# Attention stage of a macaron block: fewer visits to the values, the causal masks one by one, and the sums' copy on another engine

## The reference

```python
x = x + 0.5 * ffn(layernorm(x))        # gate and up 512 -> 4096, tanh GELU, down 4096 -> 512; weights in 4-bit codes
x = x + attention(layernorm(x))        # 16 heads of 32, causal, 2048 tokens
x = x + 0.5 * ffn(layernorm(x))        # the same weights again

# attention, per head:
scores = q @ k.T / sqrt(32) + causal
out = softmax(scores) @ v              # then out @ w_out.T + b_out over all heads
```

## Time and profile before

| | |
|---|---|
| median of the runs | 2957.84 us |
| the profiled execution | 2956.98 us, span 2955.2 us |
| PE busy | 2893.9 us, 98% of the span |
| DVE, ACT, POOL busy | 1826.2, 1051.2, 1066.9 us (62%, 36%, 36%) |
| granted TensorE clock, mean | 0.995 |
| the attention's heads | some 1263 to 1860 us of the span |

### The profile page before, as it was taken

One profiled execution on the slowest core, in us unless ns is written; L12 is line 12 of the kernel. 1 busy time (PEld: TensorE's weight loads), 2 busy tenths in 40 slices (PEclk: granted clock), 3 DMA queues, 4 the chain that ended last, 5 costly groups with the idle time before them and its releaser, 6 DMA issues. The chain is left out here.

```text
span 2955.2 us, 49495 instructions
## 1 busy us (share of the span) xinstructions
PE 2893.9 (98%) x19280; PEld 2336.1 (79%) x19280; DVE 1826.2 (62%) x3321; ACT 1051.2 (36%) x1827; POOL 1066.9 (36%) x745
## 2 busy tenths in 40 slices
PE   7999999999999999999999999899999999999999
PEld 5888888888888877867777776678888888888887
DVE  5665655565656544577777775666565655565664
ACT  4322222222222222266666664432222222222222
POOL 3322222222222214566666662332222222222221
PEclk9999999999999999999999999999999999999999
DMA  3000000000000015732232222100000000000001
GB/s 100 29 22 29 22 28 21 21 24 25 26 23 28 1 47 99 222 86 60 61 74 70 60 85 63 37 29 22 29 24 26 26 24 21 21 28 21 28 8 57
DMA packets 98630, 127.86 MB, mean 43 GB/s; under 512 B 43068, under 2 KB 51244, under 8 KB 95148
## 3 DMA queue, kind: packets, MB, share of 16 engines
q1 hardware_dynamic: 98476, 125.72, 15.1%
HBM read 96.34 MB, written 29.34 MB: 43 GB/s over the span
## 5 line engine op out<-in xcount | busy, mean ns | idle before, releaser
L59 PE MATMUL psum<-ffn_x_high,ffn_w_high 128*128 128x512 f32 x2048 | 800.0, 391 | 15.3 <-DVE ffn_gelu L466 13.2
L60 PE MATMUL psum<-ffn_x_low,ffn_w_high 128*128 128x512 f32 x2048 | 798.0, 390 | 0.0
L61 PE MATMUL psum<-ffn_x_high,ffn_w_low 128*128 128x512 f32 x2048 | 797.8, 390 | 0.0
L612 POOL TENSOR_TENSOR ffn_inner<-ffn_gelu,ffn_inner 128x512 fp32r<-128x512 f32 x256 | 346.1, 1352 | 1156.5 <-ACT ffn_inner L549 1156.5
L456 DVE SCALAR_TENSOR_TENSOR ffn_gelu<-ffn_gelu,psum 128x512 f32<-128x512 f32 x256 | 176.0, 688 | 606.8 <-ACT ffn_gelu L542 606.8
L59 PEld LDWEIGHTS psum<-ffn_x_high,ffn_w_high 128*128 128x128 f32 x2048 | 385.2, 188 | 98.8 <-DVE ffn_gelu L466 16.3
L61 PEld LDWEIGHTS psum<-ffn_x_high,ffn_w_low 128*128 128x128 f32 x2048 | 385.2, 188 | 80.3
L60 PEld LDWEIGHTS psum<-ffn_x_low,ffn_w_high 128*128 128x128 f32 x2048 | 385.3, 188 | 79.6
L59 PE MATMUL psum<-ffn_inner,ffn_w_high 128*128 128x512 f32 x1024 | 398.6, 389 | 0.2
L60 PE MATMUL psum<-ffn_inner,ffn_w_high 128*128 128x512 f32 x1024 | 398.4, 389 | 0.0
L61 PE MATMUL psum<-ffn_inner,ffn_w_low 128*128 128x512 f32 x1024 | 398.3, 389 | 0.0
(11 more groups left out here) (123 smaller groups left out, 3567.1 us busy)
## 6 DMA issues: line engine op xcount, KB each, us to landing
ffn_words<-packed SPq DMA_DIRECT2D x96, 256.0 KB
ffn_word_scales<-scales SPq DMA_DIRECT2D x96, 256.0 KB
qk_parts<-parts SPq DMA_DIRECT2D x32, 512.0 KB, 4.0
queries<-qk_parts SPq DMA_DIRECT2D x48, 256.0 KB, 4.1
keys<-qk_parts SPq DMA_DIRECT2D x48, 256.0 KB, 6.2
v_parts<-parts SPq DMA_DIRECT2D x16, 256.0 KB, 3.0
values<-v_parts SPq DMA_DIRECT2D x16, 256.0 KB, 7.7
out<-x SPq DMA_DIRECT2D x16, 256.0 KB, 2.0
```

Source lines behind the costliest of these rows:

```text
L59: pe.matmul(out, w_high, x_high, start=first, stop=False, skip_group_check=True)
L60: pe.matmul(out, w_high, x_low, start=False, stop=False, skip_group_check=True)
L61: return pe.matmul(out, w_low, x_high, start=False, stop=last, skip_group_check=True)
L612: pool.tensor_tensor(inner[:, tb % 2, m, 1, :], product[m], f32(inner[:, tb % 2, m, 0, :]), ALU.subtract)\
```

## The change

`MEETS_AT` replaces the visit behind each batch by six visits in a head: batches 0 and 1 behind slot 7, 2 and 3 behind slot 15, 4 behind 19, 5 and 6 behind 27, 7 and 8 behind 35, 9 behind 39. `quads` gets a third buffer. Each diagonal tile's mask is issued directly behind its scores. In the 15 heads of `head`, the copy out of `out_bank` moves from ACT to DVE, there behind `take_max` and `split_max` of the same slot; the last head keeps it on ACT, and keeps its ten visits.

```diff
--- before.py
+++ after.py
@@ -673,6 +673,9 @@
 
 QUADS = [i for i in range(BATCHES) if BATCH * i not in DIAGONAL_TILES]
 
+MEETS_AT = {7: (0, 1), 15: (2, 3), 19: (4,), 27: (5, 6), 35: (7, 8), 39: (9,)}
+NQUADS = 3
+
 
 
 
@@ -1288,7 +1291,7 @@
         ROWS, queries, keys, values = heads.ROWS, heads.queries, heads.keys, heads.values
         probs = sb("probs", [P, RING, TB], F32)
         heads_out = sb("heads_out", [P, NOUT, 2, P], F32)
-        quads = sb("quads", [P, 2, TB], F32)
+        quads = sb("quads", [P, NQUADS, TB], F32)
 
         start = sb("start", [P, 7], F32)
 
@@ -1377,9 +1380,9 @@
                 if kt < 4 * b:
                     last.then_inc(scores_ready, 1)
 
-            def masks(s, u):
-                for v in (u - 1, u):
-                    pe.matmul(score_bank_of(s, v)[:, 0:P], heads.ident_b[:], heads.key_mask_b[:],
+            def mask(s, u):
+                if u in DIAGONAL_TILES:
+                    pe.matmul(score_bank_of(s, u)[:, 0:P], heads.ident_b[:], heads.key_mask_b[:],
                               start=False, stop=True, skip_group_check=True).then_inc(scores_ready, 1)
 
             def value_lane(s, t, q):
@@ -1398,7 +1401,7 @@
                 c = QUADS.index(i)
                 pe.wait_ge(quad_steps, 54 * hp + 18 * (s + 1) + 3 * (c + 1))
                 for q in range(QUARTERS):
-                    last = sum_lane(quads[:, c % 2, :], q, 0)
+                    last = sum_lane(quads[:, c % NQUADS, :], q, 0)
                 last.then_inc(quads_met, 1)
 
             def meet_batch(hp, s, i, last_head=False):
@@ -1426,21 +1429,16 @@
                 if t0 + BATCH - 1 in OUT_DONE:
                     last.then_inc(out_ready, 1)
 
-            def masks_of(s, u, in_batch):
-                if u in DIAGONAL_TILES and u % 2 == 1 and (u % BATCH == BATCH - 1) == in_batch:
-                    masks(s, u)
-
             def head(hp, s):
                 for t in range(SLOTS):
                     of, u = divmod(t + AHEAD, SLOTS)
                     scores(hp, s + of, u)
-                    masks_of(s + of, u, False)
+                    mask(s + of, u)
                     heads.max_chunk(pe, hp, s + 1, t)
                     if t in ROWS_AT:
                         heads.rows(pe, hp, s + (ROWS_AT[t] not in OWN_ROWS), ROWS_AT[t])
-                    masks_of(s + of, u, True)
-                    if t % BATCH == BATCH - 1:
-                        meet_batch(hp, s, t // BATCH)
+                    for i in MEETS_AT.get(t, ()):
+                        meet_batch(hp, s, i)
 
             def project(n):
                 k = STEPS[n][1]
@@ -1464,11 +1462,9 @@
                     u = t + AHEAD
                     if u < SLOTS:
                         scores(hp, 0, u)
-                        masks_of(0, u, False)
+                        mask(0, u)
                     if t in ROWS_AT and ROWS_AT[t] in OWN_ROWS:
                         heads.rows(pe, hp, 0, ROWS_AT[t], alone=True)
-                    if u < SLOTS:
-                        masks_of(0, u, True)
                     if t % BATCH == BATCH - 1:
                         for n in STEPS_AT.get(t // BATCH, []):
                             project(n)
@@ -1485,11 +1481,18 @@
 
         @block.vector
         def _(dve):
+            def take_out(hp, s, e):
+                dve.wait_ge(out_ready, 3 * NOUT * hp + (NOUT * s + e + 1))
+                dve.wait_ge(out_stored[e], 240 * hp + 80 * (s + 1))
+                dve.tensor_copy(heads_out[:, e, :, :], out_bank[:, 0:2 * P]).then_inc(out_free, 1)
+
             def head(hp, s):
                 for m in range(SLOTS):
                     heads.take_max(dve, hp, s + 1, m)
                     if m == LAST_CHUNK[CHUNKS[m][0]]:
                         heads.split_max(dve, hp, s + 1, CHUNKS[m][0])
+                    if m in OUT_DONE:
+                        take_out(hp, s, OUT_DONE.index(m))
 
             heads.fill_ones(dve, 2)
             def scale(n):
@@ -1582,18 +1585,12 @@
                 act.wait_ge(out_stored[e], 240 * hp + 80 * (s + 1))
                 act.activation(heads_out[:, e, :, :], out_bank[:, 0:2 * P], ACT.Copy).then_inc(out_free, 1)
 
-            def take_outs(hp, s, t):
-                if t in OUT_DONE:
-                    take_out(hp, s, OUT_DONE.index(t))
-
             def head(hp, s):
                 for t in range(SLOTS):
                     of, u = divmod(t + AHEAD, SLOTS)
                     exps(hp, s + of, u)
                     if t in ROWS_AT:
                         heads.store_rows(act, hp, s + (ROWS_AT[t] not in OWN_ROWS), ROWS_AT[t])
-                    if t % BATCH == BATCH - 1:
-                        take_outs(hp, s, t)
 
             def high(n):
                 act.wait_ge(o.scaled, scaled_at(n))
@@ -1609,7 +1606,8 @@
                     if t % BATCH == BATCH - 1:
                         for n in STEPS_AT.get(t // BATCH + 1, BEHIND[:3]):
                             high(n)
-                        take_outs(hp, 0, t)
+                        if t in OUT_DONE:
+                            take_out(hp, 0, OUT_DONE.index(t))
                 for n in BEHIND[3:]:
                     high(n)
 
@@ -1626,7 +1624,7 @@
         def _(pool):
             def add_quad(hp, s, i):
                 c = QUADS.index(i)
-                total = quads[:, c % 2, :]
+                total = quads[:, c % NQUADS, :]
                 steps = 54 * hp + 18 * (s + 1) + 3 * c
                 tiles = [probs[:, (SLOTS * s + BATCH * i + j) % RING, :] for j in range(BATCH)]
                 pool.wait_ge(quads_met, 18 * hp + (6 * s + c + 1))
@@ -1641,7 +1639,7 @@
             for e in range(NOUT):
                 pool.memset(start[:, e + 1:e + 2], 0.0).then_inc(out_stored[e], 80)
             pool.memset(start[:, 5:6], 0.0).then_inc(quad_steps, 18)
-            pool.memset(start[:, 6:7], 0.0).then_inc(quads_met, 2)
+            pool.memset(start[:, 6:7], 0.0).then_inc(quads_met, NQUADS)
             for hp in range(HEADS // 3):
                 for s in range(3):
                     for i in QUADS:
```

## The result

| | us |
|---|---|
| before, median of six runs (2956.95 to 2958.70) | 2957.56 |
| after, median of six runs (2929.72 to 2930.97) | 2930.38 |
| ratio, 95% interval | 0.9908 (0.9895 to 0.9920) |
| span of the profiled execution, before and after | 2955.2, 2928.9 |

What follows compares the result with a forecast made beforehand. PE, busy 98% of the span, was taken as the bound; stretch terms and DVE's 0.10 summed to -1.09 us a head, -16.4 over 15 heads, giving 2941.5 us; range 2930 to 2955, own range 2932 to 2949.

Steps and rivals of the forecast that it cites:

- rows in mid-stretch: Behind slots 3 and 31: `rows` taken to leave the next score's weights unhidden as a visit does; only 0.10 us each saved.
- row store: ACT's store of 0.58 us between exponentials 3 and 4 delays slot 7's score: about 0.35 lost, bounds 0 and 0.58.
- B: Slots 8 to 15 of a head, 7.10 us before; predicted -0.44: visit -0.31, bubble -0.22, masks +0.09.
- D: Slots 20 to 27 of a head, 7.03 us before; predicted -0.49: visit -0.31, bubble -0.27, masks +0.09.
- E: Slots 28 to 35 of a head, 7.32 us before; predicted -0.48: visit -0.10, bubbles -0.56, masks +0.18.
- A: Slots 0 to 7 of a head, 6.32 us before; predicted +0.25: visit -0.10, row store +0.35.
- The bubble: Waits of 128-wide scores behind mask pairs, in slot 11 and behind 22, 30 and 34: all 1.05 us a head goes.
- C: Slots 16 to 19 of a head, 3.25 us before; predicted change 0.
- 1, the copy held by POOL: DVE's copies wait for POOL's additions behind slots 15, 27, 39: 1.9 us more a head, 2970, slower; chance 0.11.
- 2, ACT holding B and D as well: Exponentials hold slots 4 to 7 of each long stretch, 0.35 again in B and D: 2952; chance 0.10.
- 3, no change: Single masks lose 0.07 more per batch and three quarters of the 1.05 bubbles return: 2958; chance 0.08.
- 4, better than the sum: Row store hides, `rows` leave nothing unhidden, single masks cost only their columns: -2.00 a head, 2928; chance 0.08.

## Why the prediction was right or wrong

**The bound** was right: PE's start-to-start distances carry the time, and no other engine took over. The sum was short by 0.52 a head. The steps below say where; the largest are the rows in mid-stretch (0.30) and DVE's lateness (0.10), and the row store (0.13) goes the other way. What is left in B, D and E (0.04, 0.07, 0.04) is not traced.

**The visits**: 0.31 each was right for slots 11 and 23 (B and D came out at -0.48 and -0.56 for -0.44 and -0.49). For slots 3 and 31 I took rows in mid-stretch to leave the next score's weights as unhidden as a visit does. They don't: from the rows at 1498.12 the score starts 0.23 later, as the rows' own four matmuls take, and its chunk 0.29 behind it where 0.235 is plain. Leaving rows costs 0.06, not 0.21, so 0.25 and not 0.10 goes in A and in E. This is the largest term that I mis-sized, 0.15 in each.

**The masks**: the timeline agrees with 0.13 a single mask (0.04 to the chunk, 0.32 from the chunk on instead of 0.235) and with the four of a batch costing some 0.08 more than two pairs: slots 8 to 11 take 2.09 after, and 2.34 - 0.22 (bubble) - 0.11 (entry) = 2.01 before. **The bubble** of 1.05 went, as the masks alone show (-0.78 in B, D and E together: 1.05 less some 0.3 for the masks' own cost). What I missed is that this term holds up the others: a sum of parts gave the visits a gain that they don't have while the masks come in pairs. It did no harm to the number, since both parts were in the change.

**The row store** in A: predicted 0.35 lost, measured 0.48 (slot 7's score at 0.60 for 0.235, and its chunk at 0.35 for 0.235). I had left out that a score that waits also leaves the weights of the chunk behind it unhidden, as at the end of a visit. In A this error and the one on the rows cancel, so +0.22 for +0.25 is luck in part.

**The copy**: predicted 0.10 a head for DVE's lateness, measured 0. The margin of 0.1 in C that I worked out was too small, since the CAST lasted 0.57 and not 0.97 (POOL's additions stand elsewhere now) and the copy ran from 0.15 to 0.57 in C instead of 0.65 to 1.05. A second copy, which ends at 0.91, still fitted in. The mechanism I described is real, and the price that I gave it, up to 0.5 in a stretch, is what the copy alone costs in the kernel before, 0.32 and 0.24.

**C** lost 0.06 more than the 0 I gave it: before, slot 19's rows already came a little late for the same reason, 0.29 behind their chunk instead of 0.235. The same holds in E with single masks and ten visits, where slot 31's rows stand 0.27 behind their chunk, and 0.20 in the changed kernel: 0.07 of E's -0.74, which I had left out too.

**The rivals.** 1, the copy held by POOL: wrong. The copies, min, median and max in ns,

```profile
L1487 DVE COPY heads_out<-psum x60: 424/425/426, 1280.3 to 1759.0; 128x256 f32<-128x256 f32 x60
```

```profile
L866 DVE CAST max_parts<-minus_max x64: 170/368/1202, 1228.7 to 1758.5; 128x4 fp32r<-128x4 f32 x64
```

are alike to 2 ns. 44 of the 60 copies ran from start to end inside an addition of POOL's; the other 16, all but one of them behind slot 35, met an idle POOL and took the same. Of the 64 CASTs, 46 started during an addition, and each of these ended 24 to 30 ns after it; the other 18 took 170 to 172 ns. The Trainium skill's rule on PSUM operands (VectorE: DVE Perf Modes, "Why PSUM operands drop a tier") keeps an fp32 copy out of PSUM at single rate, without the second read port; the 44 copies agree with what the prediction drew from it. 2, ACT holding B and D as well: wrong with single masks, and what happens with pairs. 3, no change: wrong for the change. Its number fits the visits alone, for another reason: there the pairs and their bubbles are still in place. 4, better than the sum (2928): its time was nearer than my forecast, but of its three reasons only the one on the rows held; the store didn't hide and the masks weren't free.

**Outside the six stretches**: 15 heads of 1.61 are 24.2 of 27.2 us. In the profiles the first head, from its slot 3 to its slot 39, saved 2.73 where a later one saves 1.64: its first visit lay in the time at 1.2 GHz after the stage began (the granted clock reads 0.50, then 0.58 from 1267 to 1272 us before, 0.68 after), and took 1.94 us there for the 1.08 it takes later. Another 1.5 are the last head's end, open as said.

**Would I forecast otherwise?** I had half of what was needed: the rows in mid-stretch are nowhere in the trace before, and I bounded them from one side only (as costly as a visit). Rival 4 did price the other end, with 0.10 each, though by my own reading (0.21 to leave a visit) nothing unhidden would be worth 0.21 each. The low end of my own range is also added up wrongly: its terms, 5, 5 and 1.5 off 2941.5, reach to 2930 and not to 2932, and with rival 4's 3 us for the rows to 2927. That the stated range just holds the measured time owes something to luck: its end at 2930 stands half way to rival 4 and doesn't come from the terms.

## What to carry to other kernels

Joining phases on a saturated engine removes switches only if the engine that feeds it keeps pace through the longer run: price first what stands between its items (a late mask, a store), and take that out with it; each half alone may be worth nothing or be a loss. A copy moved to an engine that serves a chain in order is free where it lands in that engine's shadow, and its price is read at the first consumer behind it (here a bank's reuse by four small matmuls), not in that engine's busy share. When a stretch got longer in a change that won, look at it next: moving the rows ahead of the visit took 0.5 us off each later head, and 3 to 5 us off the whole by the ratios.

## What the runs showed of the hardware

- Four matmuls with two weight columns (the rows) between fp32 matmuls leave 0.06 us unhidden at the next ones (1498.35 to 1498.64, 0.29 for 0.235); the 32-column lanes of a visit leave 0.21.
- A score that was held by a semaphore costs 0.11 us more than the wait, at the matmul behind it (1500.22 to 1500.57, 0.35 for 0.235).
- VectorE's copy of 128x256 fp32 out of PSUM took 424 to 426 ns, in 44 cases inside an addition of GpSimd's and in 16 beside an idle GpSimd; ScalarE's took 383 to 386. A cast of 128x4 in SBUF took 170 to 172 ns with GpSimd idle, and up to 1202 ns when it started during an addition: it ended 24 to 30 ns after that addition, in 46 of 46 cases.
